# A two-layer graph network on one core: the first four tiles of column 15 taken ahead, and the kept blocks moved to the end of each column

## The reference

```python
h = relu(layernorm(x))                     # layer 0
x1 = swish((adj @ h) @ W + b)              # "first pass" over adj
x2 = swish((adj @ x1) @ W + b)             # "second pass"
x = x + x2
h = relu(layernorm(x))                     # layer 1
a_hat = adj + I
d = sum(a_hat, axis=1) ** -0.5
x = x + ((a_hat * d[:, None] * d[None, :]) @ h) @ W1.T + b1   # "third pass"
```

## Time and profile before

| what | value |
|---|---|
| median of 3 runs | 1423.94 us |
| the profiled execution, its own time | 1426.15 us |
| its span | 1424.4 us |
| TensorE busy | 1378.0 us |
| VectorE busy | 1102.3 us |
| ScalarE busy | 719.8 us |
| GpSimd busy | 72.7 us |
| first pass, until the first matmul of the second | 754.0 us |
| read from HBM | 363.27 MB |

### The profile page before, as it was taken

How to read it: one execution, slowest core, us unless ns; L and a number is a source line. 1 busy time by engine, 2 the same in 40 slices (tenths; PEclk the granted TensorE clock), 3 DMA queues, 4 the chain that set the end, 5 groups by cost and what they waited for, 6 DMA issues and landing times. The chain is left out here.

```text
span 1424.4 us, 18691 instructions
## 1 busy us (share of the span) xinstructions
PE 1378.0 (97%) x6600; PEld 648.7 (46%) x6600; DVE 1102.3 (77%) x2372; ACT 719.8 (51%) x823; POOL 72.7 (5%) x55
## 2 busy tenths in 40 slices
PE   3899999999999999999999999999999999999998
PEld 1344444444444444444444454454444444444444
DVE  7978688989889987877694767786988886888531
ACT  6575468888778776567540122222533553355100
POOL 1100000000000100000000011100000000000000
PEclk9999999999999999999999999999999999999999
DMA  9999999999999987788730112123667556654200
GB/s 395 421 402 408 403 415 413 412 410 411 399 411 374 360 363 317 309 361 331 307 149 30 52 46 68 66 67 127 273 242 316 210 199 266 275 219 193 111 15 24
DMA packets 61732, 376.34 MB, mean 264 GB/s; under 512 B 6849, under 2 KB 7234, under 8 KB 18754
## 3 DMA queue, kind: packets, MB, share of 16 engines
q1 hardware_dynamic: 55008, 363.22, 63.4%
q10 hardware_dynamic: 6626, 11.87, 2.2%
HBM read 363.27 MB, written 11.80 MB: 263 GB/s over the span
## 5 line engine op out<-in xcount | busy, mean ns | idle before, releaser
L721 PE MATMUL acc_ps<-marks,node_a 128*128 128x512 fp8e4 x944 | 358.9, 380 | 35.1 <-DVE node_a L1114 28.7
L786 PE MATMUL acc_ps<-ring,node_a 128*128 128x512 fp8e4 x1024 | 388.1, 379 | 1.2 <-DVE ring L482 1.2
L787 PE MATMUL acc_ps<-ring,node_a 128*128 128x512 fp8e4 x1024 | 388.1, 379 | 0.0
L951 ACT ACTIVATE unused<-ring 128x2048 uint8<-128x2048 uint32 x181 | 345.5, 1909 | 63.3 <-DMA ring<-adj 56.0
L722 PE MATMUL acc_ps<-marks,node_a 128*128 128x512 fp8e4 x944 | 358.8, 380 | 0.0
L1122 DVE TENSOR_SCALAR marks<-ring 128x2048 uint8<-128x2048 f32 x214 | 265.6, 1242 | 74.1 <-DMA ring<-adj 32.0
L482 DVE TENSOR_SCALAR ring<-bits 128x256 uint32<-128x256 uint32 (+1 forms) x784 | 159.5, 279 | 80.0 <-PE acc_ps L787 79.9
L721 PEld LDWEIGHTS acc_ps<-marks,node_a 128*128 128x128 f16 x944 | 92.5, 98 | 154.2 <-issue 46.4
L787 PE MATMUL acc_ps<-ring,node_b 128*128 128x512 fp8e5 x416 | 157.7, 379 | 0.0
L786 PE MATMUL acc_ps<-ring,node_b 128*128 128x512 fp8e4 x416 | 157.7, 379 | 0.0
L786 PEld LDWEIGHTS acc_ps<-ring,node_a 128*128 128x128 f16 x1024 | 100.3, 98 | 120.4 <-issue 1.7
(11 more groups left out here) (146 smaller groups left out, 1383.2 us busy)
## 6 DMA issues: line engine op xcount, KB each, us to landing
ring<-adj SPq DMA_DIRECT2D x256, 1024.0 KB, 7.8
node_b<-adj SPq DMA_DIRECT2D x49, 1024.0 KB, 12.9
marks<-adj SPq DMA_DIRECT2D x26, 1024.0 KB, 6.9
node_b<-x SPq DMA_DIRECT2D x4, 1024.0 KB, 11.1
xch<-x SPq DMA_DIRECT2D x16, 256.0 KB, 2.8
xn_scratch<-xnew ACTq DMA_DIRECT2D x16, 256.0 KB, 2.0
xch<-xn_scratch SPq DMA_DIRECT2D x16, 256.0 KB, 2.9
out<-xnew ACTq DMA_DIRECT2D x16, 256.0 KB, 3.8
```

The lines of the kernel that those rows point to most:

```text
L721: nc.tensor.matmul(acc_ps[c % 2][:, :], hi_of(node_a16, j), byte, start=(j == opens * TB), stop=False)
L786: nc.tensor.matmul(into[:, :], hi_of(node, j), byte.bitcast(E4), start=opens, stop=False)
L787: last = nc.tensor.matmul(into[:, :], lo_of(node, j), byte.bitcast(low), start=False, stop=closes)
L951: nc.scalar.activation(unused[:, :], loaded_slot(g).bitcast(U32), ACT.Sign, accum_out=nz_count[:, g:g + 1]).then_inc(counted, 1)
```

## The change

`AHEAD` gets one more entry: behind tile 4.15 the tiles 15.0 to 15.3 are loaded, marked, packed and multiplied (all four of one column, where the other entries take four columns' first tile or two columns' first two). They are holes of column 15 then: their group is packed already, so the packing of that group is left out, `LATE` gets these four tiles, and the count comparison moves from step 13 to step 14 of the third pass. The first sum saved for column 15 lies in the second half of `xch`, so SyncE's first load there waits until the sums of column 15 are whole (`nT_ready`), and the projection of column 15 moves from behind block 6 to behind block 12 of the second pass. The 12 kept blocks of columns 3 to 15 move from behind tiles 4 to 11 to behind tiles 8 to 15.

```diff
--- before.py
+++ after.py
@@ -60,7 +60,7 @@
 
 
 KEPT = 3
-KEPT_AFTER = (4, 5, 5, 6, 7, 7, 8, 9, 9, 10, 11, 11)
+KEPT_AFTER = (8, 9, 9, 10, 10, 11, 12, 12, 13, 13, 14, 15)
 COUNT_STEPS = 11
 
 
@@ -68,7 +68,8 @@
 
 
 
-AHEAD = {TC + 3: (3, 4, 5, 6), 2 * TC + 3: (13, 14), 2 * TC + 7: (11, 12), 2 * TC + 11: (9, 10), 3 * TC + 7: (7, 8)}
+AHEAD = {TC + 3: (3, 4, 5, 6), 2 * TC + 3: (13, 14), 2 * TC + 7: (11, 12), 2 * TC + 11: (9, 10), 3 * TC + 7: (7, 8),
+         4 * TC + 15: (15,)}
 AHEAD_COLUMNS = [c for ahead in AHEAD.values() for c in ahead]
 AHEAD_TILES = {c: 4 // len(ahead) for ahead in AHEAD.values() for c in ahead}
 SINGLES = [c for c in AHEAD_COLUMNS if AHEAD_TILES[c] == 1]
@@ -77,7 +78,7 @@
 
 UNSIGNED = [TC, TC + 2, 2 * TC + 1]
 LATE = list(range(TC)) + UNSIGNED + [g for g in ACT_MARKED if g >= TC]
-LATE += [c * TC + i for i in range(2) for c in sorted(AHEAD_COLUMNS) if i < AHEAD_TILES[c]]
+LATE += [c * TC + i for i in range(4) for c in sorted(AHEAD_COLUMNS) if i < AHEAD_TILES[c]]
 LATE_STEP = 6
 LATE_SLOTS = 6
 
@@ -128,6 +129,11 @@
     return range(1 if ORDER[4 * r + 1].hole else 0, 2)
 
 
+def packed_ahead(r):
+
+    return ORDER[4 * r + 3].hole
+
+
 def groups_upto(c):
     return OWN[c * TC + TC - 1] // 4 + 1
 
@@ -227,7 +233,7 @@
 def project_blocks():
 
     sizes = [sum(len(list(piece.blocks())) for piece in PIECES if piece.step == k) for k in range(2 * NC)]
-    at = [6]
+    at = [12]
     for k in range(1, 2 * NC):
         at.append(min(max(6, PROJECT_GAP - (sizes[k - 1] - at[k - 1])), sizes[k] - 2))
     return at
@@ -463,6 +469,9 @@
 
 
         def saved_x(c):
+            if c == NC - 1:
+
+                return half(xch, 1)
             return bits[:, (c * UC + UC + UC // 2) * WORDS:(c * UC + UC + UC // 2) * WORDS + CW].bitcast(F32)
 
         def saved_y(c):
@@ -530,6 +539,9 @@
                 par = k % 2
                 if k >= 2:
                     sp.wait_ge(xn_ready, k - 1)
+                if k == 1:
+
+                    sp.wait_ge(nT_ready, NC)
                 sp.dma_start(b3(half(xch, par)), x_v[:, n * CB:(n + 1) * CB, :]).then_inc(xch_in[par], 16)
                 if n >= KEPT:
                     sp.wait_ge(part_out, 16 * (n - KEPT + 1))
@@ -954,7 +966,7 @@
                         if len(AHEAD[g - 1]) == 4:
                             save_y(AHEAD[g - 1][2])
                         else:
-                            save_x(AHEAD[g - 1][1])
+                            save_x(AHEAD[g - 1][-1])
                     if g - 2 in AHEAD:
                         if len(AHEAD[g - 2]) == 4:
                             save_x(AHEAD[g - 2][3])
@@ -973,6 +985,7 @@
                         early_store(stored)
             early_out(NC - 1)
             sums_out(NC - 1)
+            early_store(NC - 1)
             sigmoid(NC - 1)
             high_part(NC - 1)
 
@@ -1123,6 +1136,10 @@
 
 
             def pack_half(r):
+                if packed_ahead(r):
+                    dve.wait_ge(pack4_ready, r)
+                    dve.sem_inc(pack4_ready, 1)
+                    return
                 first, u = (r * GT % MARK_RING) * TILE, units_of(r)
                 m = marks[:, first:first + GT * TILE].bitcast(U32).rearrange("p (g h w) -> p g h w", g=GB, h=2)
                 dve.wait_ge(marked, marked_upto((r + 1) * GT - 1))
@@ -1131,6 +1148,10 @@
                                                m[:, u[0]:, 1, :], ALU.logical_shift_left, ALU.bitwise_or).then_inc(pack4_ready, 1)
 
             def pack_again(r):
+                if packed_ahead(r):
+                    dve.wait_ge(pack2_ready, r)
+                    dve.sem_inc(pack2_ready, 1)
+                    return
                 dve.wait_ge(pack4_ready, r + 1)
                 u = units_of(r)
                 p4 = pack4.rearrange("p (g h w) -> p g h w", g=GB, h=2)
@@ -1138,15 +1159,20 @@
                                                p4[:, u[0]:, 1, :], ALU.logical_shift_left, ALU.bitwise_or).then_inc(pack2_ready, 1)
 
             def pack_last(r):
+                if packed_ahead(r):
+                    dve.wait_ge(bits_ready, r)
+                    dve.sem_inc(bits_ready, 1)
+                    return
                 dve.wait_ge(pack2_ready, r + 1)
                 u, e = units_of(r), ORDER[r * GT]
                 p2 = pack2.rearrange("p (g h w) -> p g h w", g=GB, h=2)
                 if e.ahead and e.c in SINGLES:
                     to = bits_v[:, e.c + 1:e.c + 4:2, 1, :]
-                elif e.ahead:
+                elif e.ahead and e.c in PAIRED:
                     pair = sorted((e.c, ORDER[r * GT + 2].c))
                     to = bits_v[:, pair[0]:pair[1] + 1, 0, :]
                 else:
+
                     to = bits_v[:, e.c, e.i // 2 + u[0]:e.i // 2 + GB, :]
                 nc.vector.scalar_tensor_tensor(to, p2[:, u[0]:, 0, :], 4, p2[:, u[0]:, 1, :],
                                                ALU.logical_shift_right, ALU.bitwise_or).then_inc(bits_ready, 1)
@@ -1505,7 +1531,7 @@
                 else:
                     late_check(k - NC)
                     prepare_out(k - NC)
-                if k == NC + 13:
+                if k == NC + 14:
                     compare_counts()
                 if k == NC + 15:
                     dve.wait_ge(differ_sum, 1)
```

## The result

The changed kernel takes 1432.47 us (median of 5 runs, 1430.85 to 1435.52), the kernel before 1424.12 on the same chip (5 runs, 1423.87 to 1426.92). The ratio is 1.0061, with a 95% interval of 1.0051 to 1.0072. That is 8.35 us slower, where +4.4 was forecast and 1430.9 was the top of the range.

What follows compares the result with a forecast made beforehand. Columns 4 to 6 were taken as bound by the 1 MB loads (5.9 us of waits), later columns by TensorE's work. -0.8 + 5.2 = +4.4 us turned the median 1423.94 into 1428.3, range 1426.2 to 1430.9.

Steps and rivals of the forecast that it cites:

- (1): Column 15 loses four tiles that were each used twice: 13.8 us less between 696 and 754.
- (2): Four tiles behind 4.15: columns to 6 end 13.0 later, net -0.8 us with (1); kept blocks there only trade places.
- A sign of being wrong: The prediction called itself wrong if, among other signs, the waits of column 4 shrank by over 1 us.
- ScalarE's hold at the second save: Column 5: saving the second result delays the load of 5.06, 2.9 us lost; covered by a margin of 1.2 us.
- (3): Start of column 15: TensorE stands still until 15.4 is marked, since kept_used is raised later; +5.2 us, or 4.2 with short unpack.
- The price: Start of column 15: release, unpack, count step, mark and start summed, 0.2 + 2.39 + 1.24 + 1.23 + 0.15 = +5.2 us.
- rival (c): Loads starved over 2.9 us at the second save, or cover failing in columns 7 to 14: +6.4 to 7.4, 1430.8; 12%.
- (4): Behind the first pass: later projection, features, x load, late checks and count comparison cost nothing, 1.4 us to spare at the last.
- Rival (a): No stall in column 15, because VectorE gets past kept_unpack earlier: -0.8, 1423.1 us, no change; 8%.
- Rival (b): Kept blocks and new tiles fill all 5.9 us of waits and nothing is paid: 1418.1 us, faster; 5%.

Runs made afterwards that it cites:

- The first experiment: Changed kernel with the kept blocks of column 14 alone back behind tiles 4 to 11: 1424.25 us against 1424.6, ratio 0.9998.
- the second pair: Second profiles of the changed kernel (unaltered, median 1432.52 us) and of the kernel before (unaltered, one run, 1424.2 us).
- the second profile of after: Changed kernel run again unaltered on another chip: median 1432.52 us, ratio 1.0061; the profiled run took 1431.0.
- second experiment: Changed kernel with KEPT_AFTER as before in all columns, only the tiles of column 15 taken ahead: 1425.6 us, ratio 1.0006.
- first three experiments: Changed kernel with old kept positions in column 14 (1424.25 us) or all columns (1425.6); kernel before with the new KEPT_AFTER alone (1424.23).

## Why the prediction was wrong

The direction and the stall were right, the price of the stall was not. By its own parts:

- **(1) and (2), -0.8.** The waits among the new tiles, the end of column 6 and the cover in columns 5 and 6 came within 0.9 us of the forecast. The first experiment, which keeps these parts and has no stall, stands 0.35 us below the kernel before, with 1.3 us of uncertainty to either side. But the term was read off one execution whose loads came slower than in any other profile, and no run tells it from nothing. Taking the end of column 6 less the 13.81 us, the first pair of profiles gains 1.4 us, and the second pair (361.24 against 347.07) loses 0.4.
- **A sign of being wrong that came up.** The prediction named a column 4 whose waits shrink by over 1 us. They did, from 3.48 to 0.05, but column 3's rose from 0.91 to 3.48, which is the trading of places that part (2) describes; the two columns together wait 3.5 us against 4.4. The sign was badly chosen, as it left column 3 out.
- **ScalarE's hold at the second save.** 5.06 was issued at 288.39 (forecast 289.4) and landed at 293.16 (294.2); ScalarE began to mark 5.15 at 318.44 (forecast 318.3). That mark was ready only 0.28 us before TensorE came to it, not 1.2, but the cover held.
- **(3) the place and the length of the stall.** Right: 5.18 for 5.2, with the unpack at its long value. The long value came from GpSimd's addition lying across it:

```profile
708.62 2.38 DVE L491 TENSOR_SCALAR kept_marks<-bits 128x384 uint32<-128x384 uint32 x4 [14.30 <-PE kept_ps L672]
710.92 1.20 DVE L1214 TENSOR_TENSOR count_b<-bits,count_a 128x2048 uint16<-128x2048 uint16 x1
712.16 2.36 DVE L1135 TENSOR_SCALAR marks<-ring 128x2048 uint8<-128x2048 f32 x2
```

```profile
708.79 1.27 POOL L611 TENSOR_TENSOR nT<-nT,bits 128x512 f32<-128x512 f32 x1 [5.98 <-ACT nT L907]
```

  Unpack, count step and the first of the two marks follow without a break, as summed, and the run with the kept blocks behind 14.13 shows the short value once the addition is out of the way.
- **(3) "The price", the step that failed.** I charged the stall at its own length, +5.2, and left out what TensorE does after it. The granted clock fell to its lower level behind the wait and the matmuls of 15.4 on ran 0.43 us apart: 2.7 us more in one profile, 1.4 in the other, and 2.6 by the medians with the wait filled and not filled (3.8 by the ratios). The price of this stall was about 8 by the medians (1432.47 less 1424.25), and 7.9 and 6.6 in the two profiles, not 5.2. The range had no room for it either. By the forecast's own terms (+3.0 to +5.8, and +6.4 to +7.4 for rival (c)) it would have been 1426.9 to 1431.3, not the 1426.2 to 1430.9 stated, and the measured 1432.47 is above both.

  What the trace of the kernel before had to say about it was mixed, and one trace wasn't enough. Its clock isn't at 1.00 throughout: behind TensorE's last record, which ends at 1419.31, it falls to 0.50 at 1423.23. But the one long wait inside its work, 3.24 us in column 0, was followed by matmuls 0.22 apart:

```profile
52.47 0.38 PE L721 MATMUL acc_ps<-marks,node_a 128*128 128x512 fp8e4 x1 [3.24 <-DVE node_a L1114]
52.69 0.38 PE L722 MATMUL acc_ps<-marks,node_a 128*128 128x512 fp8e4 x1
```

  The second profile of the same kernel has the same wait, and there the matmuls behind it are slow:

```profile
52.36 0.59 PE L721 MATMUL acc_ps<-marks,node_a 128*128 128x512 fp8e4 x1 [3.24 <-DVE node_a L1114]
52.74 0.63 PE L722 MATMUL acc_ps<-marks,node_a 128*128 128x512 fp8e4 x1
53.17 0.63 PE L721 MATMUL acc_ps<-marks,node_a 128*128 128x512 fp8e4 x1
```

  The Trainium skill warns of such falls (TensorE: Matmul & The Clock Gate, Part 1: idle gaps between bursts of matmuls send the clock back to its lower level, to be earned again). The traces agree for the waits of 3.75 us and more; the wait of 3.2 us in column 0 brought a fall in nine of eleven profiles and none in two.
- **(4), at nothing.** The projection, the last features and the comparison cost nothing that shows: from its first matmul of the second pass to its last matmul, TensorE took 664.2 to 665.4 us in the second profile of after and in the first and second experiment, against 665.1 before. What stands out in the first profile of after (668.35) is the wait at the start of the third pass. The gap was 1.98 in the second profile of the same kernel, 0.70, 1.81 and 1.25 in the first three experiments, and none with the late checks shifted. In the first profile of after one late load came some 1.5 us late (the 1.68 above), and the long gap isn't shown to belong to the change.
- **Rival (a)**, no stall: fell with the 5.02 us. **Rival (b)**, all waits filled: fell with the 0.6 us waits in the new first halves, and with columns 3 to 6, which took no less with late kept blocks than without. **Rival (c)**, starved loads or cover lost in columns 7 to 14: fell, although its number (1430.8) lies nearer to the measured one than mine. Columns 5 and 6 wait 0.2 us in all, and columns 7 to 14 take 346.36 us against 346.35 before.

In medians: -0.35 for the parts without a stall, +5.6 for the stall, +2.6 for the clock, 7.9 of the 8.35. The 0.5 left over is the difference between the kernel before's medians on the two chips (1424.6 and 1424.12).

## What to carry to other kernels

Price a wait of TensorE inside otherwise unbroken work twice: its own length, and what the clock takes back behind it, read from places in traces where a wait of that length ended. Take more than one execution for it: the same wait may bring a fall of the clock in one and not in the next, so put the fall into the range even where one trace is without it. Before work is moved to the end of a stage, list what is released by it and what the next stage has in hand until then; here each half of the change was harmless, and they met at the one column where one took away the cover and the other needed it. When the change leaves work out of an engine's hands, ask also who else runs beside the operations on the new path (GpSimd's addition made 1.0 us of the 5.2).

## What the runs showed of the hardware

- From 60 us to the last matmul, the granted clock fell at waits of 2.85, 3.75, 5.01 and 5.02 us, and at no wait of 1.78 us or less; nothing in between was seen there. The wait of 3.23 to 3.27 us before the matmul at some 52.3 us, which every profile has, brought a fall in nine profiles and none in two (the first of the kernel before, and the one with the late checks shifted). The fall needn't come within the wait: behind the 2.85 us it came at 1019.45, when TensorE had been at work again since 1019.00. Two waits of 5.0 us in the same kernel cost 2.7 and 1.4 us more: the clock was at 0.50 from 712.25 to 719.08 in one and from 712.32 to 715.73 in the other. No run here says why the one was dearer.
- The clock doesn't need useful work to hold: 22 f16 matmuls into a spare bank did it, and won 2.6 us back of the loss. They cost nothing, since they ended before the mark came.
- VectorE's four unpack operations took 1.39 to 1.41 us alone and 2.35 to 2.47 when an f32 addition of GpSimd (1.26 to 1.82 us) ran across their start, or began within 0.3 us of it, in all eleven profiles. Where the addition began 1.0 us behind the start of the unpack (426.73 against 425.74 in the first profile of the kernel before), the unpack kept its 1.40.
